# Moving the last step of three layer norms from VectorE to ScalarE in a six-layer decoder on one core

## The reference

```python
def _layernorm(x, axis=-1, eps=1e-05):
    m = jnp.mean(x, axis=axis, keepdims=True)
    v = jnp.var(x, axis=axis, keepdims=True)
    return (x - m) / jnp.sqrt(v + eps)
...
x = _layernorm(x + _L0_attn_ref(...))    # causal attention
x = _layernorm(x + _L0_xattn_ref(...))   # long convolution over products with the context
x = _layernorm(x + _L0_ffn_ref(...))     # ternary feed-forward
x = _layernorm(x + _L1_attn_ref(...))    # recurrent layer
x = _layernorm(x + _L1_xattn_ref(...))   # cross-attention, 16 heads
x = _layernorm(x + _L1_ffn_ref(...))     # gated feed-forward in fp8
```

## Time and profile before

| | before |
|---|---|
| time, median of 3 runs | 882.16 us (879.91 to 882.3) |
| span of the profiled execution | 880.8 us |
| PE busy | 819.1 us (93%) |
| PEld busy | 638.4 us (72%) |
| DVE busy | 694.7 us (79%), 1703 instructions |
| ACT busy | 522.0 us (59%), 1299 instructions |
| POOL busy | 295.8 us (34%), 315 instructions |

### The profile page before, as it was taken

The page is one execution under the profiler, slowest core; times in us unless marked ns, Lnnn a source line. Parts: engine busy times, 40 slices in busy tenths (PEclk is TensorE's granted clock), DMA queues, the critical chain, the costliest instruction groups (busy, mean ns, idle before and its releaser), DMA issues.

```text
span 880.8 us, 14412 instructions
## 1 busy us (share of the span) xinstructions
PE 819.1 (93%) x5004; PEld 638.4 (72%) x5004; DVE 694.7 (79%) x1703; ACT 522.0 (59%) x1299; POOL 295.8 (34%) x315
## 2 busy tenths in 40 slices
PE   6877978999999999999999999999899999999984
PEld 5654855788777778878687777876778867787863
DVE  2696786988898869986897979986897789655654
ACT  4536125646626766387644975269644679567863
POOL 1442723522444226411562133612264133311110
PEclk9897889999999999999999999999999999999998
DMA  8942010010001000100001000010000000000000
GB/s 285 368 143 86 13 37 13 1 25 13 1 1 25 25 13 2 25 13 13 13 1 37 1 13 13 1 37 1 13 1 1 13 0 1 4 11 1 13 1 24
DMA packets 37062, 28.65 MB, mean 33 GB/s; under 512 B 18688, under 2 KB 34560, under 8 KB 36608
## 3 DMA queue, kind: packets, MB, share of 16 engines
q1 hardware_dynamic: 36992, 27.74, 10.3%
HBM read 25.64 MB, written 2.10 MB: 31 GB/s over the span
## 4 chain that ended last, share of the span: by engine, by line
PE 63%; DVE 21%; issue 6%; ACT 6%; DMA 1%; POOL 1%; SPq 1%; DVEq 0%; POOLq 0%; ACTq 0%
PE bank L1320 9%; PE bank L1359 8%; PE bank L1047 6%; PE bank L1338 5%; PE bank L1348 5%; PE bank L1238 5%; PE bank L1148 2%; PE bank L1343 2%; PE bank L1118 2%; PE bank L1119 2%; DVE S L975 2%; PE bank L1186 2%; PE bank L1116 2%; PE bank L1041 2%; DVE Zc L789 1%
## 5 line engine op out<-in xcount | busy, mean ns | idle before, releaser
L1320 PE MATMUL bank<-XTE,w_xq 128*128 128x256 f32 x512 | 123.0, 384 | 1.2 <-ACT QA L664 1.2
L672 ACT ACTIVATE S<-S,mx 128x128 f32<-128x128 f32 x256 | 99.4, 394 | 41.0 <-DVE mx L978 40.6
L1359 PE MATMUL bank<-w_xo,OX 128*128 128x256 f32 x512 | 116.0, 380 | 0.0
L1320 PEld LDWEIGHTS bank<-XTE,w_xq 128*128 128x128 f32 x512 | 95.1, 192 | 18.8 <-issue 5.3
L1359 PEld LDWEIGHTS bank<-w_xo,OX 128*128 128x128 f32 x512 | 95.9, 190 | 15.5 <-issue 2.8
L389 POOL TENSOR_TENSOR rq<-vq,minus_half 128x8 f32<-128x8 f32 x32 | 53.3, 1665 | 141.3 <-DVE vq L966 141.3
L663 ACT ACTIVATE QS<-bank,per_partition_sb 128x256 f32<-128x256 f32 x128 | 60.6, 473 | 54.4 <-PE bank L1320 47.7
L975 DVE SCALAR_TENSOR_TENSOR S<-bank,rq,xmask 128x128 f32<-128x128 f32 x256 | 71.7, 343 | 15.5 <-PE bank L1338 10.2
L1338 PEld LDWEIGHTS bank<-KTX,QA 128*128 128x128 f32 x512 | 63.7, 192 | 9.9 <-issue 7.5
L286 POOL TENSOR_TENSOR prod<-XTA,ccolA 128x256 f32<-128x256 f32 x96 | 60.3, 659 | 25.4 <-PE bank L1119 17.3
L1338 PE MATMUL bank<-KTX,QA 128*128 128x128 f32 x512 | 67.9, 277 | 0.2 <-ACT OX L684 0.2
(11 more groups left out here) (223 smaller groups left out, 1849.4 us busy)
## 6 DMA issues: line engine op xcount, KB each, us to landing
xin<-in_x SPq DMA_DIRECT2D x8, 256.0 KB, 2.7
taps_sb<-in_taps SPq DMA_DIRECT2D x1, 2048.0 KB, 11.3
cnat<-in_ctx SPq DMA_DIRECT2D x8, 256.0 KB, 2.7
ccolA<-in_ctxT SPq DMA_DIRECT2D x32, 64.0 KB, 2.6
ccolE<-in_ctxT SPq DMA_DIRECT2D x16, 128.0 KB, 2.4
w_xq<-in_L_xattn_Wq SPq DMA_DIRECT2D x1, 2048.0 KB, 12.0
w_xo<-in_L_xattn_Wo SPq DMA_DIRECT2D x1, 2048.0 KB, 17.4
out_x<-X SPq DMA_DIRECT2D x8, 256.0 KB, 2.1
```

What stands on the lines that cost most here:

```text
L672: ins = nc.scalar.activation(S[:, b, seq(h)], S[:, b, seq(h)], ACT.Exp, bias=mx[:, b, h:h + 1], accum_out=sm[:, b, h:h + 1])
L1320: ins = nc.tensor.matmul(cols(EQ)[:, h], w_xq[:, k, hh * XDIM:(hh + 1) * XDIM], XTE[:, k], start=k == 0, stop=k == HALVES - 1)
L1359: ins = nc.tensor.matmul(rows(EY)[:, b], OX[:, h, b], w_xo[:, n * XGROUP + h], start=n == 0 and h == 0 and b == 0, stop=n == XKV - 1 and h ...
```

## The change

VectorE no longer runs `norm_out` for the norms c and e. It makes one small operation more for each of them, the negated mean. GpSimd, after rstd, waits for it and multiplies the two to a shift per row. ScalarE then computes X = rstd * U + shift, with scale and bias as columns, one activation per sequence, in a new step for each of the 24 norms; their places in ScalarE's order are new letters in `ORDER["act"]`, and nothing else in that order is changed. From VectorE's order the 24 letters are taken out. VectorE waits for the norm e of the group before, before it overwrites UE. The first and last norms of station a keep their form.

```diff
+        minus_mean, shift = ({s: sb(f"{n}_{s}", [GB]) for s in "ce"} for n in ("minus_mean", "shift"))
...
                 power(rstd[s][:], veps[s][:], GB, f"n{st}_rstd")
+                if st in "ce":
+                    gp.wait_ge(sems[f"n{st}_rstd"], 2 * nth(g, per, i) - 1)
+                    sig(gp.tensor_tensor(shift[s][:], minus_mean[s][:], rstd[s][:], ALU.mult), f"n{st}_rstd")
...
+            def norm_out(g, st, i, per, src):
+                x = X[g % XBUF]
+                yield
+                act.wait_ge(sems[f"n{st}_rstd"], 2 * nth(g, per, i))
+                for b in range(GB):
+                    ins = nc.scalar.activation(x[:, b], src[:, b], ACT.Identity, bias=shift[st][:, b:b + 1], scale=rstd[st][:, b:b + 1])
+                sig(ins, f"n{st}_out")
...
+                yield from norm_out(g, "c", 0, 2, UC)
...
+                yield from norm_out(g, "c", 1, 2, UC)
+
+            def output(g):
+                yield from norm_out(g, "e", 0, 1, UE)
...
                 order(ins)
+                if st in "ce":
+                    nc.vector.tensor_scalar(minus_mean[s][:], mv[s][:, :, 0], -1.0, None, ALU.mult)
                 sig(nc.vector.tensor_scalar(veps[s][:], mv[s][:, :, 1], eps, None, ALU.add), f"n{st}_stats")
...
                 norm("c", UC)
-                yield
-                dve.wait_ge(sems["nc_rstd"], nth(g, 2, 0))
-                norm_out("c", UC, x)
...
                 norm("c", UC)
-                yield
-                dve.wait_ge(sems["nc_rstd"], nth(g, 2, 1))
-                norm_out("c", UC, x)
...
                 dve.wait_ge(sems["e_y"], nth(g, XKV, XKV - 1))
+                if g > 0:
+                    dve.wait_ge(sems["ne_out"], nth(g - 1))
                 sig(nc.vector.tensor_tensor(UE[:], x[:], rows(EY), ALU.add), "e_u")
                 dve.wait_ge(sems["e_u"], nth(g))
                 norm("e", UE)
-                yield
-                dve.wait_ge(sems["ne_rstd"], nth(g))
-                norm_out("e", UE, x)
```

More of the change, by code:

```diff
@@ L605, in ternary_ffn @@
                     sig(nc.scalar.activation(Q3T[:, b].rearrange("p k s -> p (k s)"), as_bf((C0, C1)[b]), ACT.Copy), "c_q3Tc")
+                yield from norm_out(g, "c", 0, 2, UC)
             def recurrent(g):
-                K1, R, _, _, XTC, _, C0, C1 = recurrent_buffers(g)
+                K1, R, _, _, XTC, UC, C0, C1 = recurrent_buffers(g)
                 yield
@@ L687, in _ @@
             together(ORDER["act"], s=set_up(), a=station_a(front, ffn), c=station_c(ternary_ffn, recurrent), r=recurrent(0), q=station_q(keys, queries),
-                     x=each_group(lambda g: scores(g, 0)), y=each_group(lambda g: scores(g, 1)))
+                     x=each_group(lambda g: scores(g, 0)), y=each_group(lambda g: scores(g, 1)), o=each_group(output))
         @block.vector
@@ L1386 @@
     "dve": (
[L1387 to L1391, removed]
@@ L1392 @@
-        "xaqcaxcaqcoaqaoayqayaaxaaaxqcccaaacaycaacayacacaccqyaxyxcycqaxycxcccyaxyccqoaxqoaayqccqycxaxcqccycac"
-        "yacxcxcqyaxyaxaqyxyoxoaqayaxyxaqaaxyxayqaaxyaxyaaaaaooaaaaaaaaa"
+        "aasssassaaasaassaaaasaasasaasaqasaasaasaqaqacacacccccaccacaqaccaaqaaaaaqaaaaaaaaararararararaccraacc"
+        "acqacccaaqcacaayaaxaacaayaacaaaaqayxcyccacxaacxacycqycacaxaxacycxqaxayacaaacccaccaaoacaqacaqaaxaqaya"
+        "qcxacyacqxacxaccaycyacaacaaqaacaxyxyaacqacyaxyaaxacaacaacaacaacaaqaayaacaycaqaoqxqcxccycacqcaycacaxa"
@@ L1394 @@
+        "acxyayaqxaaxacycyqaacxaxcaccaqacacqaaxqaayaaqaacaaxacayaaaqoaacccxcacxcaycyaccaaaqyxaayxacaacqycyxac"
+        "ccaxccayqxccxqayoqaaqcaacaaacaaacaaacaacaaqacaxyaxccyaxaxacayaaqycxaaxacayaqycccacacxaqcaxcaqoaqaayq"
+        "ayaaxaaaxqcccaaacaycaacayacaaccqyaxyxcycqaxycxcccyaxyccqoaxqaayqccqyxaxcqccycacyacxcxqyaxyaxaqyxyoxa"
+        "qayaxyxaqaaxyxayqaaxyaxyaaaaaoaaaaaaaaa"
     ),
     "act": (
-        "sassaasaasassssscqsqqcqacscaacccscaaccccarrrqqqqcaaacqacqacqcccqcaqcqccqycxyyccycxyxxyqxaqyxacaaaqyc"
@@ L1397 @@
[L1397 to L1401, removed]
+        "sassaasaasassssscqsqqcqacscaacccscaaccccacrrrqqqqcaaarcqacqacqcccqcaqcqccqycxycyccycxyxxyqxaqyxaccaa"
@@ new lines @@
+        "aqycxqcyxqxcycaxqcyqcxycxccccoccxcyqcxqxayaqxqyaqayqacacyqxaaqcxcyqxayqaaaqcyxacycxyaxcqcxqxcyycccyy"
+        "cyccxocqaqaxyaxqqaycqcaaqxyqaaxyqxcyxqycqacxqyacaxacyaqxccqaxycxccxycqqxcxqcyqoccaqaxqyaxyqacycqaayx"
+        "acaqyxqcqycxyaccxayacyxacqcyaqxccxcyxccacoqcqxyxqycqxycaxqaxqcyxaqcaxyqaayqcxaaqcxyqcyxyxacqcaacaqay"
+        "ccycxaxcxoyqcxyqcycqqqyqqyccyqxaxaqycxqycxyqcxyaccxycxycqxcayqxycayaocxcayxaqcxcqyccyqxqyqxqyqxqcyxa"
+        "xqayqaxyqyxaxqyxyqoyaxaxqayxqaxyxyqaxqayxyaxyaaxyaxyaxayoaaaaaaa"
```

## The result

The change made the kernel slower by 0.6%: 886.64 us (883.15 to 889.29, 9 runs) against 881.68 us (878.55 to 882.62, 9 runs of the kernel before beside them), a ratio of 1.006 with a 95% interval of 1.0042 to 1.0078. The profiled executions differ by less, 883.6 against 880.8 us: the one of before ran 34.1 of its first 155 us at the lower granted clock, the one of after 20.4, and at 160 us TensorE was 2.5 us further on in the one of after. The forecast was 883.8 us with "no change" as the likeliest; the measured time lies inside the range, at the place of the second rival.

A forecast was written before the change was run, and what follows sets the result against it. TensorE, busy 93% of the span, was taken to set the time, with VectorE second. Costs of 3.2 + 0.8 less gains of 2.4 added 1.6 us to the 882.2 median: 883.8 us, 8 in 10 within 878.5 to 888.0.

The forecast's parts named there:

- the second rival: ScalarE dense stretches: pairs ahead of needed work cost 0.6 us at twelve places; 4.8 us more, 887.0 us; chance 0.34.
- The five named costs: Five places without slack where the moved steps would delay TensorE, together 3.2 us.
- 133 us: Group 0, recurrent norm: new step delays line 588 and so TensorE's ternary product; cost 0.7 us.
- 179: Group 1, ternary norm, at 179 us: TensorE already waits for X, which comes later; cost 0.55 us.
- 740: Group 5, cross-attention norm, at 740 us: new step ahead of line 605 pushes its result; cost 0.5 us.
- 807: Group 6, cross-attention norm, at 807 us: pair inside a dense ScalarE stretch; cost 0.90 less 0.14 slack, 0.76 us.
- 862: Last group's norm, at 862 us: TensorE stood still there, so the full added latency counts; cost 0.7 us.
- At about seven other places ... I take 0.8 us in all.: Places where ScalarE's next instruction stood within 0.9 us: 0 to 0.9 us each, mostly covered by TensorE's queue; 0.8 us total.
- The gain: Pairs leaving VectorE at 517 to 569 us win 1.8 us, at 652 and 578 us 0.3 each; together 2.4 us.
- ScalarE becomes the bound: Slack behind ScalarE below 0.9 us at most of 24 places; twelve cost 0.6 us each; 887.0 us; chance 0.34.
- Relief carries further: VectorE's other waits shrink too, its queue being shorter everywhere; 879.4 us, or 877.8 if costs halve; chance 0.21.
- the two marks I had set: TensorE's idle time, 160 to 840 us: below 9 us means wrong on the fast side, above 16 on the slow.

The follow-up runs named there:

- the longer cover: The changed kernel with 80 instead of 56 small TensorE products ahead of the last group's transposes: 885.34 us, ratio 1.0042.

## Why the prediction was right or wrong

- **The five named costs.** 133 us: 0.7 forecast, 0.84 to 1.13 in the kernels that have the step there. 179: 0.55, measured 0.60. 740: 0.5, measured 0.58. 807: 0.76, measured 0.61. 862: 0.7, measured 0.69. In sum 3.2 against 3.3 to 3.6. Each fell to 0.00 or 0.01 when its step went back. The reading of these from the slack behind ScalarE held, with two reservations. At 807 us the slack was read at 823 us, and the wait came at 809.8, so that the size fits by chance. And three of them cost a second time a few us later, at 747, 813 and 865 us, 0.9 us together, which the sum had at nothing.
- **"At about seven other places ... I take 0.8 us in all."** This is the step of the sum that failed. 296 us (+1.23), 394 us (+0.74), 218 us (+0.25) and 213 us (+0.23) make 2.4 to 2.5. Two things were wrong in it. The push was bounded by 0.9 us, two starts 0.45 us apart. That holds where an activation follows and overlaps the pair; ahead of a table load the whole 1.09 us count, and so does the wait for the shift, 0.15 us, as ScalarE had had no wait there. And "mostly covered by TensorE's queue" was read from the absence of a wait of TensorE. At 296 us the eviction came 0.11 us before it was taken, behind a ScalarE without a gap: the slack was to be read from the end of the last activation before TensorE's product, five us behind the step, and not from the waits.
- **The gain.** Its size was about right (1.8 forecast at 560 us, 2.2 measured at 552 and 560, with 0.36 more at 545; 0.3 at 652 us, 0.72 measured; 0.3 at 578 us, nothing seen). For most of it the reason was wrong. I had put it down to 2.6 us that leave VectorE. Leaving all 24 steps out gives 0.08 and 0.49 us at 552 and 560; one step moved gives all of those, and a useless GpSimd product gives the first 0.57 with no work taken away. It is the order in which a VectorE and a GpSimd instruction start. That a forecast of the right size came from the wrong mechanism is chance. At 545 and 656 us relief does explain the gain: 0.36 and 0.59 of it are there with the steps left out.
- **Latency terms.** Product with wait 0.30, measured 0.27. Negated mean 0.1, measured 0.08. The pair 1.02, measured 1.09. VectorE's relief 17 to 21 us busy, measured 16.7; ScalarE's +27, measured +23.5: 48 x 0.564 counts the two of a pair apart, and they overlap each other and what stands before them.
- **Which case came.** With the smaller changes the places give 7.0 us of costs and 3.1 of gains, +3.9, where 4.0 - 2.4 = 1.6 were forecast. The costs were too small by 3.0: 1.7 in the "seven other places", 0.9 in what is paid a second time, 0.4 in the five named. The rival "ScalarE becomes the bound" gave 7.2 us of costs and 887.0, which is nearly the time, and its mechanism, the pair ahead of an eviction that TensorE needs next, is what stands at most of the cost places. What it had wrong is their number: it wanted slack below 0.9 us at most of the 24 seats, and no more than nine show a cost; with seven of them back, the other seventeen cost 0.7. "Relief carries further" is refuted by the steps left out, whose whole gain is 1.3 us. TensorE's idle time between 160 and 840 us, 13.1 us, lay between the two marks I had set.
- **What stays open.** How often the stretch near 852 us or at the tail's fp8 products runs at the lower clock, and so how much of the 5.3 us it is; the longer cover does not decide it, neither by its times nor by its trace. Also what sets the 0.25 to 0.49 at 218 us; no run was made for it.

## What to carry to other kernels

Before moving work to an idle engine, follow for each seat that engine's queue behind it to its next real gap, and ask who takes a result on the way with less slack than the step is long, whether or not a wait shows there; the load in total said nothing here (leaving 21 us off VectorE was worth 1.3 us, while about nine seats out of 24 cost some 7 us). Then follow it on to the next taker: three of the seats were paid for twice. Judge a mixed change by seat: with five steps of the stretch where VectorE had the chain, it was 0.27% faster than before instead of 0.6% slower. And where two engines hold each other up, as VectorE and GpSimd do here, a gain may hang on which of two instructions starts first by less than half a microsecond, so it should be expected to turn with the next edit.

## What the runs showed of the hardware

- **VectorE beside GpSimd.** One instruction of VectorE (R, 128x512) takes 0.69 us if it starts before GpSimd's product and 1.98 to 2.42 us if it starts 0.03 to 0.47 us after it. An unused product of two numbers per row (0.46 us) put in front of a GpSimd instruction shortened four VectorE products from 4.20 to 3.12 us.
- **The clock of TensorE.** The granted clock is 1.00 over 160 to 840 us in both kernels, but short stretches at the lower of the two levels (granted 0.50, 1.2 instead of 2.4 GHz: fp8 products 0.43 us apart instead of 0.21) come in some executions and not in others, behind a wait of TensorE that the kernel before has as well: near 254 us (1.75 and 0.29 us of waiting ahead of it), near 619 (1.85) and near 852 (0.63 and 1.57; in the kernel with the steps left out 0.62). They cost 1.25 to 1.68 us each. The tail's fp8 products had one in two executions, behind waits of 1.63 and 1.25 us, 1.67 and 1.69 us. With waits of 0.94 and 0.97 us at the tail, as before, no execution had it there, nor had the three with the tail's step on ScalarE in which the stretch came near 852 us. Two profiled executions of kernels this close must be compared place by place, as their spans differ by such stretches: 884.3 against 880.8 us for a kernel whose moved steps cost 2.0.
- **The table load.** 1.28 us, and it begins only when the activation ahead of it has ended (290.62 + 1.09 = 291.71, load at 291.72), where an activation starts 0.09 us before that end (133.13 against 133.22).
